# A two-layer decoder on one core: the query projections of the first cross attention as three products of rounded high and low parts, through eight PSUM banks

## The reference

```python
head_scale = jnp.exp2(-jnp.arange(1, N_HEAD + 1, dtype=jnp.float32))
q = (x @ W_q).reshape(Bq, T1_, N_HEAD, D_HEAD).transpose(0, 2, 1, 3)
k = (context @ W_k).reshape(Bq, T2_, N_HEAD, D_HEAD).transpose(0, 2, 1, 3)
v = (context @ W_v).reshape(Bq, T2_, N_HEAD, D_HEAD).transpose(0, 2, 1, 3)
scores = jnp.einsum('bhqd,bhkd->bhqk', q, k) * atten_scale
scores = scores + bias[None, None, :, :] * head_scale[None, :, None, None]
attn = jax.nn.softmax(scores, axis=-1)
out = jnp.einsum('bhqk,bhkd->bqhd', attn, v).reshape(Bq, T1_, N_HEAD * D_HEAD)
return out @ W_out + b_out
```

## Time and profile before

| | |
|---|---|
| median of three runs | 1433.26 us (1430.25 to 1434.88) |
| the profiled execution | 1429.79 us, span 1428.0 us |
| TensorE matmul busy | 1356.4 us, 95% of the span |
| VectorE, ScalarE, GpSimd busy | 1065.1, 864.0, 767.4 us |
| mean granted TensorE clock | 0.984 |
| the folds and the loop (lines 624, 744) | between 54 and 94 us from the start of the span |

### The profile page before, as it was taken

The page is one execution under the profiler, slowest core; times in us unless marked ns, Lnnn a source line. Parts: engine busy times, 40 slices in busy tenths (PEclk is TensorE's granted clock), DMA queues, the critical chain, the costliest instruction groups (busy, mean ns, idle before and its releaser), DMA issues.

```text
span 1428.0 us, 25410 instructions
## 1 busy us (share of the span) xinstructions
PE 1356.4 (95%) x9220; PEld 1012.2 (71%) x9220; DVE 1065.1 (75%) x2128; ACT 864.0 (61%) x1849; POOL 767.4 (54%) x431
## 2 busy tenths in 40 slices
PE   7889999999999999999998987899999999999898
PEld 4648888888888888888866754555556556555687
DVE  6458778888777887778844677677777777776787
ACT  4437667666667666667623553566666666665575
POOL 5026443334444444442260291588888888885363
PEclk9899999999999999999999999999999999999999
DMA  3132222211212222221150123446446446420331
GB/s 85 61 91 52 57 57 57 55 43 36 49 52 58 57 51 57 57 57 36 43 151 15 57 64 80 115 104 139 106 101 138 110 95 139 94 66 1 87 105 45
DMA packets 71803, 104.39 MB, mean 73 GB/s; under 512 B 14670, under 2 KB 54934, under 8 KB 71550
## 3 DMA queue, kind: packets, MB, share of 16 engines
q1 hardware_dynamic: 60062, 91.39, 25.6%
q10 hardware_dynamic: 11616, 11.38, 3.0%
HBM read 63.65 MB, written 2.11 MB: 46 GB/s over the span
## 4 chain that ended last, share of the span: by engine, by line
PE 79%; DVE 11%; DMA 3%; ACT 2%; issue 2%; SPq 1%; POOL 1%; ACTq 0%; DVEq 0%; POOLq 0%
PE PS L701 9%; PE PS L1104 6%; PE PS L715 6%; PE PS L689 5%; PE PS L690 5%; PE PS L691 5%; PE PS L1118 5%; PE PS L717 5%; PE PS L716 5%; PE PS L1084 5%; PE PS L1043 3%; PE PS L1049 3%; DMA inv_kept<-row_inv 2%; PE PS L744 2%; DVE QO_area L1399 2%
## 5 line engine op out<-in xcount | busy, mean ns | idle before, releaser
L1233 POOL TENSOR_TENSOR QO_area<-QO_area,prob_a 125x896 f32<-125x896 f32 x150 | 315.1, 2101 | 22.7 <-ACT prob_a L1325 3.2
L867 ACT ACTIVATE HL<-PS 125x512 fp32r<-125x512 f32 (+1 forms) x384 | 206.8, 539 | 177.8 <-PE PS L701 160.7
L959 DVE TENSOR_TENSOR HL<-PS,HL 125x512 fp32r<-125x512 f32 (+1 forms) x384 | 238.0, 622 | 74.6 <-ACT HL L867 53.5
L1399 DVE TENSOR_REDUCE QO_area<-PS 112x1 f32<-112x500 f32 x384 | 238.9, 670 | 60.3 <-PE PS L1084 60.2
L1325 ACT ACTIVATE prob_a<-PS 125x448 f32<-125x448 f32 x384 | 187.5, 540 | 103.9 <-PE PS L1104 100.5
L774 POOL TENSOR_TENSOR HL<-ctx_area,ones 125x512 fp32r<-125x512 f32 (+1 forms) x64 | 93.1, 1454 | 247.3 <-PE PS L717 189.3
L715 PE MATMUL PS<-HL 125*128 125x512 f32 (+1 forms) x384 | 155.7, 405 | 2.4 <-DVE HL L959 2.0
L689 PE MATMUL PS<-HL 128*128 128x500 f32 x336 | 153.1, 456 | 4.7 <-DVE HL L929 3.9
L1104 PEld LDWEIGHTS PS<-HL 98*125 98x125 f32 x768 | 102.9, 186 | 71.4 <-ACT prob_a L1325 37.9
L877 ACT ACTIVATE prob_a<-prob_a,neg_max 128x500 f32<-128x500 f32 x192 | 135.5, 706 | 26.7 <-DVE neg_max L951 25.4
L1084 PE MATMUL PS<-HL 96*112 96x500 f32 x384 | 129.4, 408 | 17.9 <-DVE QO_area L1399 15.3
(11 more groups left out here) (262 smaller groups left out, 2743.3 us busy)
## 6 DMA issues: line engine op xcount, KB each, us to landing
HL<-prob_b SPq DMA_DIRECT2D x128, 187.5 KB, 4.0
ctx_area<-in_ctx_T SPq DMA_DIRECT2D x16, 750.0 KB, 13.4
ctx_area<-in_ctx SPq DMA_DIRECT2D x16, 750.0 KB
HL<-ctx_area SPq DMA_DIRECT2D x64, 187.5 KB, 3.8
inv_area<-in_ctx_T SPq DMA_DIRECT2D x8, 750.0 KB, 4.1
prob_a<-in_ctx_T SPq DMA_DIRECT2D x8, 750.0 KB, 4.7
inv_area<-inv_kept ACTq DMA_DIRECT2D x16, 256.0 KB, 3.5
ctx_area<-in_L_ffn_W SPq DMA_DIRECT2D x16, 256.0 KB, 3.4
```

The lines of the kernel that those rows point to most:

```text
L867: nc.scalar.activation(pH[k % 3][0:KC, 0:width(g)], PS[0:KC, 2 + k % 3, 0:width(g)], ACT.Copy)\
L959: nc.vector.tensor_tensor(pL[k % 3][0:KC, 0:width(g)], PS[0:KC, 2 + k % 3, 0:width(g)], pH[k % 3][0:KC, 0:width(g)].bitcast(fp32), ALU.sub ...
L1233: nc.gpsimd.tensor_tensor(late_acc[b % 2], before, late_p[n % LATE_P], ALU.add).then_inc(m["padd"], 1)
L1399: nc.vector.tensor_reduce(late_part[b % 2][:, u // NKB, u % NKB:u % NKB + 1], PS[0:2 * S, u % NKB, 0:KB], AX, ALU.max).then_inc(m["mx"], 1)
```

## The change

The fp32 product of a head becomes three fp32r products. The folds are kept as a high part (`foldH`, the copy of ScalarE, which now goes to a rounded buffer) and a low part (`foldL`, one more VectorE instruction for each of groups 0 to 3). The normalised stream gets a high part (`qH[1]`, ScalarE) and a low part (`qL[1]`, VectorE). Both live in buffers that are free at that time. The loop goes through eight banks instead of four: head h uses the pair 2 * (h % 4), and waits for the head four before it. Heads 2 and 3 wait for the copies of all fold groups, since these lie in banks 4 to 7.

```diff
+        foldH, foldL = (halved(128, NH * 128).rearrange("p (h c) -> p h c", h=NH) for i in range(2))
...
-        def norm_vector(dve, n):
+        def norm_vector(dve, n, between=None):
...
+                if between and h == 0:
+                    between()
...
         def fold_tensor(pe, first, last):
...
-                wait_past(pe, fold_ev, k, 4)
+                if k >= 4:
+                    pe.wait_ge(fold_lo, k - 3)
...
+        def fold_low(dve, k):
+            dve.wait_ge(fold_ev, k + 1)
+            nc.vector.scalar_tensor_tensor(fold_heads(foldL, k), PS[:, 4 + k % 4, :].rearrange("p (h c) -> p h c", h=4),
+                                           XD ** -0.5, fold_heads(foldH, k).bitcast(fp32), ALU.mult, ALU.subtract)\
+                .then_inc(fold_lo, 1)
+
         def fold_scalar(act):
             for k in range(8):
+                if k == 4:
+                    for h in range(2):
+                        act.wait_ge(xn_ready, 2 * 1 + h + 1)
+                        nc.scalar.activation(half_of(qH[1], h), half_of(XN, h), ACT.Copy).then_inc(xn_hi, 1)
...
             pe.wait_ge(xn_ready, 2 * n + 2)
-            pe.wait_ge(fold_ev, 4)
+            pe.wait_ge(fold_lo, 4)
+            pe.wait_ge(xn_hi, 2)
             for h in range(NH):
-                p = h % 2
-                if h >= 2:
-                    pe.wait_ge(m["qpa" if p == 0 else "qpd"], h // 2)
-                for a in range(2):
-                    mm = nc.tensor.matmul(PS[:, 2 * p + a, 0:HALF], qk_fold[:, h, :],
-                                          XN[:, a * HALF:(a + 1) * HALF], start=True, stop=True)
+                p = h % 4
+                if h >= 4:
+                    pe.wait_ge(m["qpa" if h % 2 == 0 else "qpd"], h // 2 - 1)
+                elif h >= 2:
+                    pe.wait_ge(fold_ev, 8)
+                for i, (w, x) in enumerate(((foldH, qH[1]), (foldL, qH[1]), (foldH, qL[1]))):
+                    if h == 0 and i == 2:
+                        pe.wait_ge(xn_lo, 2)
+                    for a in range(2):
+                        mm = nc.tensor.matmul(PS[:, 2 * p + a, 0:HALF], w[:, h, :], half_of(x, a),
+                                              start=i == 0, stop=i == 2)
                 mm.then_inc(m["qp"], 1)
...
         def cross_vector(dve, chain):
             m = xa0
+            for k in range(1, 4):
+                fold_low(dve, k)
+            for h in range(2):
+                dve.wait_ge(xn_hi, h + 1)
+                nc.vector.tensor_tensor(half_of(qL[1], h), half_of(XN, h), half_of(qH[1], h).bitcast(fp32),
+                                        ALU.subtract).then_inc(xn_lo, 1)
...
-            norm_vector(dve, 1)
+            norm_vector(dve, 1, between=lambda: fold_low(dve, 0))
```

More of the change, by code:

```diff
@@ L273, in decoder_kernel @@
         fold_mm, fold_ev, vo_out = sem("fold_mm"), sem("fold_ev"), sem("vo_out")
+        fold_lo, xn_hi, xn_lo = sem("fold_lo"), sem("xn_hi"), sem("xn_lo")
         names = ("q q0h q0 qp qpa qpd kspl vspl scores biased mx exp tr trh trc pv inv norm out").split()
@@ L626, in fold_tensor, with fold_heads @@
                 mm.then_inc(fold_mm, 1)
+        def fold_heads(x, k):
+            return x.rearrange("p (g a) c -> p a g c", a=2)[:, k // 2 % 2, 4 * (k % 2):4 * (k % 2) + 4, :]
+        def fold_low(dve, k):
[3 more added lines that the diff above has]
+                .then_inc(fold_lo, 1)
         def fold_scalar(act):
             for k in range(8):
+                if k == 4:
+                    for h in range(2):
+                        act.wait_ge(xn_ready, 2 * 1 + h + 1)
+                        nc.scalar.activation(half_of(qH[1], h), half_of(XN, h), ACT.Copy).then_inc(xn_hi, 1)
                 act.wait_ge(fold_mm, k + 1)
                 if k < 4:
-                    dst = qk_fold.rearrange("p (g a) c -> p a g c", a=2)[:, k // 2 % 2, 4 * (k % 2):4 * (k % 2) + 4, :]
+                    dst = fold_heads(foldH, k)
                 else:
@@ L845, in cross_scalar @@
                 for a in range(2):
-                    ps = PS[:, a, 0:HALF].rearrange("p (b s) -> p b s", b=HB)
+                    ps = PS[:, 2 * (h % 4) + a, 0:HALF].rearrange("p (b s) -> p b s", b=HB)
                     u, w = tile_columns(h)
@@ L917, in cross_vector @@
                 for a in range(2):
-                    ps = PS[:, 2 + a, 0:HALF].rearrange("p (b s) -> p b s", b=HB)
+                    ps = PS[:, 2 * (h % 4) + a, 0:HALF].rearrange("p (b s) -> p b s", b=HB)
                     u, w = tile_columns(h)
```

## The result

| | before | changed |
|---|---|---|
| median | 1434.01 us (10 runs) | 1422.22 us (10 runs) |
| profiled execution, span | 1429.79, 1428.0 us | 1420.15, 1418.3 us |

The ratio is 0.9923 (95% interval 0.9901 to 0.9945): the changed kernel is 11 us faster (8 to 14), where 6.0 us were forecast. It was measured twice more, beside other runs: 0.9938 (0.9915 to 0.9961) and 0.9940 (0.9916 to 0.9963). The mean of all its 23 runs is 1422.35 us, that of the 134 runs of the kernel before in the sessions after the first 1431.9 us (1432.0 with the first one's ten), with standard errors of 0.5 and 0.3. So the effect is **9.6 +- 0.6 us**. The 6.0 us of the forecast lie outside this. (Four runs, of four different kernels, stand hundreds of us above all others and are left out of every mean.)

What follows compares the result with a forecast made beforehand. TensorE was taken as the bound, busy 1356.4 of 1428.0 us. The loop ending 6.0 us earlier, with preparations and copies costing nothing, gave 1433.3 - 6.0 = 1427.2 us; range 1423.0 to 1431.0.

Steps and rivals of the forecast that it cites:

- The fp32r matmuls: In the projection loop: one fp32r matmul of 448 columns per 0.2025 us at the high clock, 0.373 at the low.
- The loop ends: Loop's last matmul done at 87.6 us against 93.6 before, 6.0 us less, with the start unchanged at 65.5.
- no head waits for a copy: In the loop, eight banks leave 3.6 us for a copy of 1.28 us, so this wait was costed at nothing.
- the preparations: Added VectorE and ScalarE steps ahead of the loop, done by 63.7 us, hidden behind the folds; cost 0, at most 0.3.
- The low parts of the folds: VectorE instructions ahead of the loop, taken at 0.75 us each for 512 columns, between bounds of 0.65 and 0.76.
- The banks alone: In the loop, ending the wait for a bank without changing the number type is worth about 1 us.
- The bias loads: Behind the loop: SyncE issues them until 82.6 us, bias is wanted at 93.6, so over 7 us in hand.
- rival (c): Clock rises earlier in the loop or doesn't fall in the handover: gain 7.6 to 10.1, 1423.2 to 1425.7 us; chance 0.12.
- isolated gap: Rival for the loop: matmuls 189 instead of 202.5 ns apart, gain 7.1, 1426.2 us; chance 0.03.
- The main loop is bound by TensorE, so it starts 6.0 us earlier and ends 6.0 us earlier: Behind the projection loop: its whole 6.0 us gain was to pass through the main loop to the kernel's end.
- All that follows waits for semaphores of the work before it, not for a time: Premise for everything behind the loop: later work moves forward with the work before it, by 6.0 us.
- (b): Clock comes up late: the loop's low stretch lasts 6.8 us more, gain 2.9, 1430.4 us; chance 0.13.

## Why the prediction was wrong

**Right:** every term up to the main loop. The fp32r matmuls stand 0.203 us apart at the high clock (taken: 0.2025) and 0.374 at the low clock (0.373). The loop ends at 87.7 (87.6), no head waits for a copy, the preparations are done at 62.9 (63.7), and the first bias instruction is at 93.67 (93.6). The low parts of the folds took 0.63 to 0.68 us each; the 0.75 taken was too long, and most lie below the lower bound of 0.65 as well, but they are off the path. The banks alone shorten the loop by 1 us, as said. The bias loads were in time. Filling the handover gave back 1.6 us up to 120 us, as rival (c) had it. The Trainium skill (TensorE: Matmul & The Clock Gate, section Back-to-back issue gap) states an isolated gap of N / 2.4 + 2.5 ns at full clock, 189 ns here; in this stream, where each matmul has a weight load of its own, the measured 203 ns is 14 ns longer, so the trace does not agree with it.

**Wrong:** the step "The main loop is bound by TensorE, so it starts 6.0 us earlier and ends 6.0 us earlier", and with it the sum of 6.0 us; 9.6 +- 0.6 were measured. The premise "All that follows waits for semaphores of the work before it, not for a time" leaves out the clock. The program behind the loop is not bound by a constant rate: it has low stretches of the clock near its handovers, their number and length differ between executions, and one of 10.2 us cost 5 us. The prediction weighed this for the two stretches next to the loop (rivals (b) and (c)), but not for those behind 750 us, in which the same kernel's two profiles differ by 8 us. That 9.6 us lie among the gains of rival (c) is luck: the profile after has both low stretches that (c) does without. It also took for granted that a shift of the loop's end reaches the kernel's end one to one, while 3.0 us of added work in the kernel before changed its time by 0.2 +- 0.6 us.

**Shown:** the loop's 5.9 us; that the fall of the clock at 98 us comes from the idle handover; that the kernels differ by 5.4 +- 1.1 us, as the loop, when both handovers are filled; that the time does not follow the loop's length one to one in the kernel before. **Argued only:** where the excess arises. Eight profiles are of kernels with split products and an unfilled handover, eight of kernels with an fp32 loop and no preparations. From the end of the loop to the end of the kernel the first take 4.4 +- 1.1 us less. The last handover has 2.5 +- 0.9 of this (42.6 to 43.8 us, one of them 45.7, against 43.0 to 49.7), the stretch that is from 889 to 932 us in the kernel before has 1.1 +- 0.5, and no other part more than 0.4. That fits in size, but each kernel has one or a few executions there. What the last handover takes goes with its low stretches. The three of the 20 profiles that have one of 10.2 us over its beginning take 48.0 to 49.7 us, and one of these three has the preparations. The five with 3.4 us of low clock 38 us or more behind its beginning and no such long one take 45.3 to 46.6. The other 12, with one low stretch of 6.8 us, take 42.6 to 44.6. The filled kernel before is among the last, with 42.6; the filled changed kernel has 45.3. **Open:** why the low stretches of the fp32 kernels without preparations would fall badly more often, even at the same place as a kernel with them (1431.9 against 1428.5), and how filling one handover at 94 us saves 4.7 us where its own stretch gives 1.6. So the step that failed is known, and the cause of the 3.7 us is not.

Of the versions tried that compute the whole reference none beats the changed kernel measurably (filled: 1421.8 +- 0.8; one repeat more of head 15: 1421.5 +- 0.4).

## What to carry to other kernels

At the high clock an fp32 matmul of 448 columns costs 0.75 us and three fp32r products of it 0.61 us here, so splitting pays wherever the parts can be made under other work; then look at the banks, because shorter products make the copy the bound (eight banks were worth 3 us of the loop with the products and 1 us of it without). When a stage is moved by a few us in a program with idle handovers, expect the end to move by the same amount only within some 4 us, and profile the kernel before more than once to see its own range. Where a difference under 0.5% is to be explained, fill the idle time of TensorE in both kernels and compare those.

## What the runs showed of the hardware that was not expected

The clock's low stretch at 61 to 71 us is absent in five of the 20 profiles: the 40 records of the folds then take 3.98 us instead of 6.2. A stage that no edit touches (the last handover) took 42.6 to 49.7 us in the 20 profiles, and how long it took went with the place and length of the low stretches in it and just ahead of it. The time of a run falls by about 1 us for each 0.001 of mean granted clock, and the runs of the kernel before range over 0.015 of it (0.975 to 0.990).
